# First layer of a four-layer network in one block: gated networks entered from the attentions' last batches, two batches of the second attention rotated in the first network's turns

## The reference, cut to what matters

```python
def _layer(x, wqkv, qs, ksc, wo, lg, lb, w1, b1, w2, b2):
    h = shift_token(x)                      # second half of the features from the token before
    q, k, v = jnp.split(h @ wqkv, 3, axis=-1)            # 8 heads of 64
    q = l2norm(q) * qs
    k = l2norm(k) * ksc
    q, k = rotary_xpos(q, k)
    o = local_attention(q, k, v)                         # windows of 64, look back one
    x = x + o @ wo
    h = shift_token(x)
    h = (h - mu) / jnp.sqrt(var + 1e-05) * lg + lb
    a, g = jnp.split(h @ w1 + b1, 2, axis=-1)            # 341 wide each
    return x + (a * jax.nn.gelu(g, approximate=False)) @ w2 + b2
for l in range(2):
    x = _layer(x, wqkv[l], q_scale[l], ...)
x = _layernorm(x_before + x)
```

## Time and profile before

| | |
|---|---|
| time, median of 3 runs | 1761.07 us (1760.69 to 1762.39) |
| the profiled execution's own time | 1756.33 us |
| its span, first to last instruction | 1754.5 us |
| granted TensorE clock, mean over the span | 0.927 |
| busy: PE, DVE, ACT, POOL | 86%, 57%, 49%, 36% |
| first layer (attention 0 to network 1) | about 59 to 542 us of the span |

### The profile page before, as it was taken

One profiled execution on the slowest core, in us unless ns is written; L12 is line 12 of the kernel. 1 busy time (PEld: TensorE's weight loads), 2 busy tenths in 40 slices (PEclk: granted clock), 3 DMA queues, 4 the chain that ended last, 5 costly groups with the idle time before them and its releaser, 6 DMA issues. The chain is left out here.

```text
span 1754.5 us, 31069 instructions
## 1 busy us (share of the span) xinstructions
PE 1509.9 (86%) x11186; PEld 1104.7 (63%) x11187; DVE 1004.8 (57%) x2367; ACT 860.9 (49%) x1888; POOL 636.9 (36%) x712
## 2 busy tenths in 40 slices
PE   4689978799987899996839999899987999778996
PEld 3356656466664566775827787788876576545664
DVE  6656536665466789996035554366655222435555
ACT  5455544556456867773424444544443233235552
POOL 3387702877240767772230000100013602411113
PEclk8789989899989889998969999999997999879998
DMA  8300000000001565544334000000000111300000
GB/s 228 111 7 19 13 7 2 13 13 13 13 1 27 87 80 77 77 61 111 84 89 134 1 0 1 1 1 1 1 1 1 46 45 32 36 4 2 2 2 25
DMA packets 75920, 64.45 MB, mean 37 GB/s; under 512 B 25627, under 2 KB 63050, under 8 KB 75790
## 3 DMA queue, kind: packets, MB, share of 16 engines
q1 hardware_dynamic: 65790, 54.32, 14.9%
q0 software_dynamic: 3072, 6.30, 1.8%
q10 hardware_dynamic: 6928, 2.12, 0.6%
HBM read 48.88 MB, written 9.58 MB: 33 GB/s over the span
## 5 line engine op out<-in xcount | busy, mean ns | idle before, releaser
L1315 POOL TENSOR_TENSOR inject<-delta_x,b_rows 128x512 f32<-128x512 f32 x128 | 160.2, 1277 | 65.2 <-DVE delta_x L1612 37.6
L1639 DVE TENSOR_TENSOR_SCAN state<-bank,inject 128x512 f32<-128x512 f32 x128 | 149.9, 1206 | 7.5 <-issue 5.2
L2072 POOL TENSOR_TENSOR ve<-mv,eps 128x1 f32<-128x1 f32 x32 | 6.1, 190 | 335.9 <-DVE mv L2220 335.9
L1544 ACT ACTIVATE bank<-delta,a_neg 128x255 f32<-128x255 f32 x256 | 108.9, 472 | 6.8 <-DVE state L1639 6.1
L3334 DVE TENSOR_REDUCE top<-bank 128x2 f32<-128x512 f32 (+1 forms) x96 | 61.8, 686 | 72.4 <-PE bank L3036 51.6
L2181 ACT ACTIVATE Z<-bank 128x512 f32<-128x512 f32 x64 | 34.7, 595 | 128.7 <-PE bank L2134 128.7
L2158 ACT ACTIVATE U<-bank 128x512 f32<-128x512 f32 x128 | 74.6, 593 | 40.8 <-PE bank L2095 39.7
L611 POOL TENSOR_TENSOR rotated<-rot_cos,rot_sin 128x512 f32<-128x512 f32 x56 | 70.8, 1269 | 52.6 <-DVE rot_sin L917 52.6
L1419 PEld LDWEIGHTS bank<-tabs,by_token 128*128 128x128 f32 x512 | 68.7, 198 | 25.2 <-issue 15.1
L617 POOL TENSOR_TENSOR inv_norm<-sum_sq,neghalf 128x16 f32<-128x16 f32 x28 | 82.0, 2929 | 4.2 <-POOL sum_sq L615 0.3
L654 PE MATMUL bank<-wqkv,hT 128*128 128x512 f32 x128 | 68.7, 667 | 14.0 <-ACT hT L815 11.3
(11 more groups left out here) (565 smaller groups left out, 4142.8 us busy)
## 6 DMA issues: line engine op xcount, KB each, us to landing
b_rows<-rows_dram SPq DMA_DIRECT2D x32, 512.0 KB, 8.7
v<-v SPq DMA_DIRECT2D x32, 130.0 KB, 2.3
slots<-zero SPq DMA_DIRECT2D x10, 256.0 KB, 3.6
rows<-slots SPq DMA_DIRECT2D x10, 256.0 KB, 4.1
moe_w<-in_L_ffn_rg_dram SPq DMA_DIRECT2D x1, 2048.0 KB, 8.4
moe_w<-in_L_ffn_ru_dram SPq DMA_DIRECT2D x1, 2048.0 KB, 13.6
wqkv<-in_L_ffn_wqkv_dram SPq DMA_DIRECT2D x2, 768.0 KB
slots_out<-y SPq DMA_DIRECT2D x8, 160.0 KB, 2.1
```

The source lines that it names most:

```text
L1315: pool.tensor_tensor(dB[:, n % R, :, :], dx[:, :, seq(n)], both(b_all[:, q % 4, n % CH, :]), ALU.mult).then_inc(s.inject.sem, 1)
L1544: last = act.activation(dA[n % RD][:, c, 1:L], delta[:, c, i * L + 1:(i + 1) * L], ACT.Exp, scale=a_neg[:, c, k:k + 1])
L1639: dve.tensor_tensor_scan(flat(h[:, n % R, :, :]), flat(dA[n % RD]), flat(dB[:, n % R, :, :]), 0.0, ALU.mult, ALU.add).then_inc(s.state.sem, 1)
```

## The change

The four blocks become one (`first_layer`), with the code of attention and network turned into functions that hold one engine's steps each. The steps of a batch stay what they were. Semaphores count on through both layers (`behind`). What moves:

1. **Entry into a network.** Turns -3 to 2 of network l are placed inside attention l's last turn and its closing steps, on every engine.
2. **Early work for attention 1.** In turns 3 to 8 of network 0 stand six projections, squares and rotations of attention 1 (half-tiles q = 0 to 5, of batches 0 and 1); POOL finishes each with four instructions, one turn later. q = 6 and 7 come in attention 1's prologue, which has no other projection of batches 0 and 1, no table and no clearing. PE projects them into banks 6 and 7.
3. **No barrier** between the four parts; the two tables of `rope` for layer 1 are made on POOL behind attention 0's share; the four DMAs of scales stand together at the head of the block.
4. Buffers: the network's `u` and `both` lie in `x_tok`, `z` and `zn` in `prob`. A few semaphores of the expert stages come from the pools, which hold 54 instead of 44.

```diff
+    def finish_early(pool, q):                       # in local_attention
+        i, m = divmod(q, 4)
+        pool.wait_ge(s.turned.sem, s.turned.at(i - 2, m + 1))
+        pool.wait_ge(s.sind.sem, s.sind.at(i, m + 1))
+        pool.tensor_tensor(rot[:, i, m, :], rc[:, m % 2, :], rs[:, m % 2, :], ALU.add).then_inc(s.added.sem, 1)
+        pool.wait_ge(s.sums.sem, s.sums.at(i, m + 1))
+        pool.tensor_scalar(ss[:, m, :], ss[:, m, :], 1e-24, None, ALU.max).then_inc(s.clipped.sem, 1)
...
+        pool.tensor_tensor(rn[:, m, :], ss[:, m, :], net.neghalf[:, 0:LH], ALU.pow).then_inc(s.inv_norm.sem, 1)
...
+        pool.tensor_tensor(of, of, rn[:, m, :].unsqueeze(2).to_broadcast([P, LH, LDH]), ALU.mult).then_inc(s.roped.sem, 1)
...
+    def early_projection(pe, q):
+        i, m = divmod(q, 4)
+        if q >= 2:
+            pe.wait_ge(s.sind.sem, s.sind.at(0, q - 1))
+        pe.wait_ge(s.h_built.sem, s.h_built.at(i, 1))
+        pe.matmul(O[m % 2], hT[:, i, tok(m // 2)], net.wqkv[l][:, ...], start=True, stop=True).then_inc(s.qk_ps.sem, 1)
...
         def run(i, p, ahead, behind, mlp=None):      # on_tensor; mlp given for the last batch alone
             shifted(i, p, 0)
+            if mlp:
+                pe.wait_ge(s.v_ready.sem, s.v_ready.at(B - 1, TPB))
+                mlp(-2)
             if behind:
                 turn_output(i - 1)
             shifted(i, p, 1)
+            if mlp:
+                mlp(-1)
...
             mix(i, p, 0)
+            if mlp:
+                pe.wait_ge(s.exped.sem, s.exped.at(B - 1, 4))
+                mlp(0)
...
             mix(i, p, 1)
...
-                runs(pe, run)
-                turn_output(B - 1)
-                output(B - 1)
+        runs(pe, run, mlp)
+        mlp(1)
+        turn_output(B - 1)
+        if l == 0:
+            mlp(2)
+        output(B - 1)
+        if l == 1:
+            written(pe, B - 1)
+            mlp(2)
...
+def first_layer(nc, net, io):
...
+            @block.gpsimd
+            def _(pool):
...
+                for t in mlp0.TURNS:
+                    mlp(t)
+                    if t >= EARLY + 2:                # EARLY = 2, LAST = 8
+                        att1.finish_early(pool, t - EARLY - 2)
+                for q in range(LAST - EARLY - 1, 8):
+                    att1.finish_early(pool, q)
+                att1.on_gpsimd(pool)
...
+            @block.tensor
+            def _(pe):
+                mlp = mlp0.tensor_turn(pe)
+                att0.on_tensor(pe, mlp)
+                for t in range(3, B):
+                    mlp(t)
+                    if t == 3:
+                        att0.written(pe, B - 1)
+                        att1.early_projection(pe, 0)
+                    att1.early_projection(pe, t - EARLY)
+                mlp(LAST)
+                mlp0.banks_free(pe)
...
+            @block.scalar
+            def _(act):
+                mlp = mlp0.scalar_turn(act)
+                att0.on_scalar(act, mlp)
+                for t in range(2, B):
+                    if t >= EARLY + 1:
+                        att1.early_square(act, t - EARLY - 1)
+                    mlp(t)
+                    if t == EARLY or t == EARLY + 1:
+                        att1.early_shift(act, t - EARLY)
+                att1.early_square(act, LAST - EARLY - 1)
...
+            @block.vector
+            def _(dve):
+                mlp = mlp0.vector_turn(dve)
+                att0.on_vector(dve, mlp)
+                for t in range(3, B + 1):
+                    mlp(t)
+                    att1.early_rotation(dve, t - EARLY - 1)
...
```

More of the change, by code:

```diff
@@ L1065, in _ @@
-                turns(turn)
+                att0.clear(pool)
+                mlp0.clear(pool)
+                att0.on_gpsimd(pool)
+                att1.tables(pool)
+                mlp = mlp0.gpsimd_turn(pool)
+                for t in mlp0.TURNS:
[5 more added lines that the diff above has]
+                att1.on_gpsimd(pool)
```

1329 lines of the change are left out of this document (729 added, 600 removed).

## The result

The changed kernel takes 1722.52 us (median of 4 runs, 1721.35 to 1723.30) against 1761.73 before (4 runs, 1760.69 to 1765.06): a ratio of 0.9774, 95% interval 0.9757 to 0.9791. It is 39.2 us faster. The profiled execution took 1722.82; its gain on that of before is 33.5 in span and in time.

What follows compares the result with a forecast made beforehand. Joints bound by waits, the network's middle by PE, attention 1's opening by DVE and POOL. Terms -7.5 + 8.4 - 16.8 - 4.1 + 0.7 - 6.7 = -26.0 gave 1735.0 us, range 1727 to 1748.

Steps and rivals of the forecast that it cites:

- B: Turns 3 to 8 of network 0, gaining attention 1's early work: DVE becomes the bound; cost +8.4 us, bounds +5 and +12.
- A: Attention 0's last batch's first score to network 0's turn 3: 37.96 us falls to 30.5, gain 7.5, bounds 9.5 and 4.
- F: Entry into network 1, attention 1's last batch's first score to turn 3: 38.20 us falls to 31.5, gain 6.7.
- the step from the profiled execution to the median: Whole kernel: the median lies 4.74 us above the profiled execution, so 1730.3 profiled becomes 1735.1.
- C: Attention 1's prologue, network 0's last residual to first score: 28.40 us falls to 11.6, gain 16.8, bounds 18 and 13.
- D: Attention 1's first turn: 26.57 us before, 22.5 forecast with POOL's finishes late; gain 4.1, bounds 6 and 0.
- The Trainium skill's rule on SBUF: POOL's finishes: two-SBUF-input DVE operations exclude POOL; none early, so powers take 1.67 us; at 2.01, D would be 1.4.
- E: Head of attention 0: two more scale DMAs ahead of the tables delay the first rotation; +0.7 us, bounds 0 and 1.
- denser PE, higher clock: Rival: PE at full speed through prologue and first turn, waits in A and F fill; -37 us, half-way 1729.5; chance 0.10.
- POOL's powers of network 0: Rival: in network 0 powers wait behind POOL's finishes, delaying normalising; price 2 to 9 us, middle 1741; chance 0.13.
- The joints overlapped: Opposite rival: joints do not overlap, A and F give only the barrier, 0.7 us each; 1748; chance 0.05.
- The clock rose: Opposite rival: PE's new waits from network 0's turn 4 on drop the granted clock; 1765 us, slower; chance 0.03.

Runs made afterwards that it cites:

- e1: The kernel before, unchanged, run again; median 1760.70 us under this label.
- e2: The changed kernel, unchanged, run again; 1721.63 us, 0.9795 of the kernel before.
- e9: Changed kernel with the edits of e6 and e8, and network 1's turn 2 cut in two around attention 1's last output; 0.9782 of the kernel before.
- e6: Changed kernel with ACT's first early square behind its turn 3 of network 0, not ahead of it; median 1720.63 us.
- e8: Changed kernel with the adds of q = 6 and 7 on DVE instead of POOL; attention 1's first turn 0.51 us shorter, at 20.17.
- e7: Changed kernel with layer 1's two scale DMAs issued behind attention 0's exchange of values, attention 0 waiting only for its own; stretch A took 31.85 us.
- e4: Changed kernel with early projections, squares, rotations and finishes of q = 0 to 5 behind network 0's last turn; 13.5 us slower than e2 by medians.
- e3: Changed kernel with both networks' turns ahead of turn 3 put back behind the attention's last output; 17.9 us slower than e2 by medians.
- e5: Kernel before plus unread matmuls in PE's idle time at the networks' starts and ahead of attention 1's first projection; 2.4 us faster by medians, 0.9985.

## Why the prediction was right or wrong

The sign was right, and so were most mechanisms; not the bound of B, and not the waits in A and F. The size was short by a third. Two steps failed. The largest is the term of the waits in A: 4.1 us were summed, 2.0 of them with no named waiter, and 1.38 were measured; F repeated it. The other is the step from the profiled execution to the median. The profiled execution was forecast at 1730.3 and took 1722.8, 7.5 less, by the terms; adding 4.74 to it made another 5.0.

On "A to scan" the gain is 34.7 for the first pair of traces and 36.3 between e1 and e2. By medians it was 39.2, 38.3 and 32.8 in three jobs, 36.8 in the mean. So no gain outside the first layer shows, and of the 39.2 some 3 are the scatter of executions.

The forecast against e2, where the clock is full throughout:

- **A**, entry into network 0: forecast 30.5, measured 26.83. This is the largest miss, 3.7. The sum was 26.4 of work and 4.1 of waits. PE's work is 25.45, 1.0 less, and the waits are 1.38, 2.7 less: 0.52 for batch 6's residual and 0.86 for batch 1's normalising, the one wait that the prediction named with a mechanism (1.1). The 2.0 for the table load, the output's copies and semaphores had no chain behind them, and none of it appeared: the load lies beside `up(0)` and `mix`. The profiled changed kernel hides a part of this miss, since a stretch at the lower clock puts 1.7 on top.

The two waits of e2 in A, on PE:

```profile
241.33 1.11 PE L741 MATMUL bank<-v,prob 128*128 128x65 f32 x8 [0.52 <-DVE x_work L1034]
...
243.92 0.41 PE L1235 MATMUL bank<-tabs,hT 128*128 128x128 f32 x2 [0.86 <-DVE xn L1304]
```

- **F**, entry into network 1: forecast 31.5, measured 28.86, the same error of size. The two waits that tell it from A, for the output's copies and for the residual behind it, were forecast at 0.9 and measured as 0.80 and 0.52; e9 moved work into them and got 1.06 back.
- **B**: forecast +8.4, measured +7.6. The first gap was right to 0.04, and e6 shows its cause as the prediction had it. The later gaps were 5.71, 5.43 and 5.03 where 6.0, 5.9 and 5.1 were forecast, since DVE didn't bound them; PE waits 0.34 at turn 5.
- **C**: 11.6 forecast, 10.9 measured, within its bounds; PE is busy 9.48 of it.
- **D**: 22.5 forecast, 20.7 measured. The mechanism and its size were right: the second turn of rotated keys was forecast 7 us into the turn and came at 7.26 (7.24 in e2), a gain of 3.9. The chain of finishes ended 6.34 into the turn, 6.0 forecast; POOL's pitch was 4.31 and not 4.44, since the next add begins where the scaling ends, but B and C were shorter too, so PE saw nothing of that. What the sum left out is the clock behind this wait, which it had only in its bound of 6. From the keys to `mix` PE was busy throughout in the kernel before, at the lower level, and took 4.32; at full clock it takes 2.79, 0.31 of it a wait. That is 1.5, and the rest of the turn, from `mix` on, gives 0.4 more.

The stretch from the keys to `mix`, in the kernel before and in the changed one:

```profile
333.98:338.30 4.32, 4.32 (x9) 2.21 (x9) 1.37 (x3) 1.68 (x3) 4.17 (x5) 0.50 0.00 0
```

```profile
312.19:314.98 2.79, 2.48 (x8) 1.17 (x9) 1.03 (x2) 1.80 (x4) 2.64 (x4) 1.00 0.00 0
```

- **Steady turns** kept 20.3 as forecast (20.28), so at 20.7 there was little left to gain in D.
- **The Trainium skill's rule on SBUF** (page "SBUF — State Buffer", section "SBUF: two separate sides") had 2.7 at stake. None of the early DVE steps has two SBUF inputs, and POOL's powers stood at 1.67 in all eight finishes. Where e8 puts a DVE add with two such inputs beside POOL, POOL's clip takes 0.68 instead of 0.24, and the add, begun beside POOL's scaling, takes 1.53, where two of the kind took 1.29 together. By that rule, the traces agree, in both directions.
- **E**: +0.7 forecast. Measured +0.65 to 0.8 from the second scale DMA to the first rotation (e7), so right. At the start of the last batch it is +0.4 between the means (233.4 and 232.9), of single values that scatter by 2.4.
- **The shift to the median**: the 4.74 by which before's median lay above its profiled execution was added to the changed kernel too. For the changed kernel it was -0.3, 1.6 and 3.9, for before 4.7 and 3.9, for e4 7.0, for e3 -0.8. It is mostly where in the spread a single profiled execution happened to fall, no property of a kernel; over all 13 kernels traced here it is 2.5 in the mean. Without it the forecast would have been 1730.3, inside the range but still 7.8 above.

In sum: without E the terms of the forecast make 26.7 on "A to scan". A missed 3.7, F 2.6, D 1.8, B 0.8 and C 0.7, in all 9.6, and 26.7 + 9.6 is the 36.3 of the traces. The rival "denser PE, higher clock" was the one that came true, nearly to its far end of -37 and not half of the way. That its sum was met so closely is in part luck: A and F gave 11.1 and 9.4 where its bounds had 9.5 and 8.5, and B cost 7.6 where it had 5. It had 0.10 because its clock and its filled waits were taken for one unlikely thing. e5 shows that in A and F they are two: the clock alone gives 0.9 there, the filled waits nearly all.

The other rivals are out. POOL's powers of network 0 didn't stand behind finishes: PE waits 0.34 at turn 5. The joints overlapped. The clock rose.

## What to carry to other kernels

A stage's filling chain costs next to nothing (0.86 us here) once another stage's matmuls stand between its links and each piece of cover is about as long as a link; price what remains link by link, and put no lump on top for "semaphores and copies" that has no named waiter. When work is moved into another loop's turns, look at the first turn alone: an operation placed one position too early there costs a wait that no later turn shows (3.3 us here, for moving one line). And put a forecast against a median with the spread of executions as its error, instead of carrying over the distance of one profiled execution. Before an experiment moves a DMA or a wait, look at what stands behind it on the waiting engine: e7 moved two and lengthened another stage's entry.

## What the hardware showed

- The granted clock of the same instructions differs from execution to execution. In three traces of the one changed kernel the stretch A had clocks of 0.94, 1.00 and 1.00 and took 28.53, 26.83 and 26.84, with the same two waits of 0.5 and 0.9 us.
- Keeping PE busy through a dependent chain raised the clock from 0.87 to 1.00 and shortened the stretch by only 0.9 of 38 us. There the low clock was mostly a symptom of the waits. Behind the wait for the keys in D, where PE had work throughout, the same clock cost 1.5 of 4.3 us.
- Jobs on three chips differed by 6 us in the same kernel (before: 1759.95, 1760.25 and 1766.45), more than the mends of e9 bring. With one job to a chip, chip and job can't be told apart. Kernels that are to be compared at this size have to share a job.
